# Attention weights normalised by ScalarE, six key heads of eight split

## What is computed

```python
q = rope(rmsnorm(x @ Wq.T))        # 32 query heads of 128, 32 rows per batch element
k = rope(rmsnorm(x @ Wk.T)); v = x @ Wv.T          # 8 key heads
kc = k_cache[block_table].reshape(bsz, 512, 8, 128)  # 16 pages of 32 keys
vc = v_cache[block_table].reshape(bsz, 512, 8, 128)
k_all, v_all = concat(kc, k), concat(vc, v)          # 544 keys
scores = q @ k_all * SCALE                           # 4 query heads share a key head
scores = where(valid, scores, -1e30)
o = softmax(scores) @ v_all
x = x + o @ Wo.T
```

## Time and profile before

| | us |
|---|---|
| median of three runs | 2377.89 (2377.67 to 2379.62) |
| the profiled execution | 2378.1 |
| its span | 2376.3 |
| TensorE busy | 2278.0 (96%) |
| VectorE busy | 1795.4 (76%) |
| ScalarE busy | 1299.5 (55%) |
| GpSimd busy | 1172.7 (49%) |
| normalising by GpSimd (L1089), 512 instructions | 536.3 |
| exponentials by ScalarE (L1193), 512 instructions | 383.8 |
| low halves of the keys by VectorE (L1248), 320 instructions | 260.4 |

### The profile page before, as it was taken

How to read it: one execution, slowest core, us unless ns; L and a number is a source line. 1 busy time by engine, 2 the same in 40 slices (tenths; PEclk the granted TensorE clock), 3 DMA queues, 4 the chain that set the end, 5 groups by cost and what they waited for, 6 DMA issues and landing times. The chain is left out here.

```text
span 2376.3 us, 52345 instructions
## 1 busy us (share of the span) xinstructions
PE 2278.0 (96%) x16384; PEld 1964.1 (83%) x16384; DVE 1795.4 (76%) x3535; ACT 1299.5 (55%) x2647; POOL 1172.7 (49%) x1254
## 2 busy tenths in 40 slices
PE   6889999999995999999999999999999997999998
PEld 6777777777774899999999999999999996888887
DVE  6861799999996788888888888888888886422222
ACT  5632788888874555555555555555555554311111
POOL 5410344444443577777777777777777774000000
PEclk9999999999998899999999999999999998999999
DMA  6633233333324788888888888888888885743442
GB/s 237 219 99 91 75 110 111 111 106 93 111 89 138 254 291 294 290 292 286 291 279 290 287 292 287 299 290 294 278 281 292 290 294 179 226 135 98 127 135 62
DMA packets 447145, 493.28 MB, mean 208 GB/s; under 512 B 95317, under 2 KB 390229, under 8 KB 438742
## 3 DMA queue, kind: packets, MB, share of 16 engines
q1 hardware_dynamic: 410198, 357.98, 47.2%
q0 software_dynamic: 36864, 134.23, 16.1%
HBM read 399.83 MB, written 92.27 MB: 207 GB/s over the span
## 5 line engine op out<-in xcount | busy, mean ns | idle before, releaser
L1089 POOL TENSOR_TENSOR att_probs<-att_probs,att_inverse 128x512 f32<-128x512 f32 x512 | 536.3, 1047 | 287.3 <-DVE att_inverse L1285 282.7
L1193 ACT ACTIVATE att_probs<-att_probs,att_low 128x544 f32<-128x544 f32 x512 | 383.8, 750 | 516.2 <-DVE att_low L1272 451.0
L1150 PE MATMUL att_o<-att_probs_t,att_values 128*128 128x128 f32 x4096 | 540.9, 275 | 0.0
L1272 DVE CUSTOM_DVE_ANT_0 att_probs<-att_score,att_mask,att_batch_cols 128x544 f32<-128x544 f32 x512 | 400.0, 781 | 138.1 <-PE att_score L1115 99.5
L1150 PEld LDWEIGHTS att_o<-att_probs_t,att_values 128*128 128x128 f32 x4096 | 497.7, 192 | 0.0
L1281 DVE COPY att_probs_t<-att_turn 128x512 f32<-128x512 f32 x512 | 350.8, 685 | 1.2 <-PE att_turn L1130 1.2
L1075 POOL DMA_INDIRECT att_values<-L_cond_v_cache,att_v_rows_of x256 | 284.0, 1109 | 82.0 <-POOL att_v_rows_of L1071 49.7
L1115 PE MATMUL att_score<-att_keys_raw,att_queries_raw 128*128 128x288 f32 (+1 forms) x1024 | 290.8, 407 | 28.1 <-DMA att_queries_raw<-q_t 25.9
L1130 PE MATMUL att_turn<-ident,att_probs 128*128 128x128 f32 x2048 | 311.4, 275 | 1.2 <-POOL att_probs L1089 0.9
L784 PE MATMUL proj_proj<-x3t_hi,proj_w_hi 128*128 128x512 f32 x640 | 266.7, 417 | 6.7 <-DVE proj_w_lo L844 6.7
L1248 DVE TENSOR_TENSOR att_keys_lo<-att_keys_raw,att_keys_hi 128x384 fp32r<-128x384 f32 (+1 forms) x320 | 260.4, 814 | 16.7 <-ACT att_keys_hi L1186 16.7
(11 more groups left out here) (133 smaller groups left out, 3982.0 us busy)
## 6 DMA issues: line engine op xcount, KB each, us to landing
att_keys_raw<-L_cond_k_cache SPq DMA_DIRECT2D x1024, 128.0 KB
q_t<-proj_q_out SPq DMA_DIRECT2D x32, 1024.0 KB, 3.9
att_queries_raw<-q_t SPq DMA_DIRECT2D x64, 512.0 KB
o_t<-att_heads_out SPq DMA_DIRECT2D x64, 512.0 KB, 6.7
out_o_raw<-o_t SPq DMA_DIRECT2D x32, 1024.0 KB, 5.6
maps_even<-L_cond_weight SPq DMA_DIRECT2D x8, 1024.0 KB, 12.7
maps_odd<-L_cond_weight SPq DMA_DIRECT2D x8, 1024.0 KB, 16.3
w_nat<-L_cond_Wq SPq DMA_DIRECT2D x8, 1024.0 KB, 5.3
```

Source lines behind the costliest of these rows:

```text
L1089: nc.gpsimd.tensor_tensor(probs[:, k, 0:L], probs[:, k, 0:L], inverse[:, k:k + 1].to_broadcast([P, L]), ALU.mult).then_inc(probs_ready, 1)
L1150: last = nc.tensor.matmul(o, values[j][:, t, h * D:(h + 1) * D], probs_t[m % 2][:, t * P:(t + 1) * P], start=(t == 0), stop=False, skip_gr ...
L1193: nc.scalar.activation(probs[:, k, :], probs[:, k, :], ACT.Exp, bias=low[k][:, 0:1], scale=-1.0, accum_out=total[k][:, 0:1]).then_inc(exp_ ...
L1272: nc.vector.tensor_tensor_reduce(out=probs[:, k, :], in0=score_ps[:, LEFT:LEFT + KEYS], in1=mask[j][:], scale=batch_cols[j][:, h:h + 1], s ...
```

## The change

ScalarE normalises a head's 512 columns, with the inverse as the scale of a copy (`normalise`), behind its high half of that head and ahead of new_part and keep_o. GpSimd keeps the gathers and the new keys' group, for which it waits on the inverse once in four heads. Two heads of a batch element stay native and not four; the six others are split. The halves so hold 6 of 8 heads, the pages are cut into six pieces (five of three pages and one of two), and with the queries there are seven; ScalarE begins with piece 0 behind head 1 and VectorE behind head 2. The release of the keys' buffer follows `NATIVE`.

```diff
--- before.py
+++ after.py
@@ -940,10 +940,10 @@
     GH = 4
     RING = 8
     PAIRS = B // 2
-    NATIVE = 4
-    ACT_FROM, DVE_FROM = 4, 5
+    NATIVE = 2
+    ACT_FROM, DVE_FROM = 1, 2
     SPLIT = HK - NATIVE
-    PARTS = [slice(0, 3), slice(3, 6), slice(6, 9), slice(9, 13), slice(13, NPP + 1)]
+    PARTS = [slice(0, 3), slice(3, 6), slice(6, 9), slice(9, 12), slice(12, 15), slice(15, NPP + 1)]
     NP = len(PARTS)
     FIRST = NPP // 2 + 1
     LEFT = 512 - FIRST * PSIZE
@@ -1084,11 +1084,9 @@
 
                             pool.wait_ge(o_done, i * N + j * HK)
                         load((j + 1) % 2, i * 2 + (j + 1), h - 3)
-                    pool.wait_ge(inverse_ready, i * N + n + 1)
-                    k = n % RING
-                    nc.gpsimd.tensor_tensor(probs[:, k, 0:L], probs[:, k, 0:L], inverse[:, k:k + 1].to_broadcast([P, L]),
-                                            ALU.mult).then_inc(probs_ready, 1)
                     if n % GH == GH - 1:
+                        k = n % RING
+                        pool.wait_ge(inverse_ready, i * N + n + 1)
 
                         heads = slice(k - GH + 1, k + 1)
                         nc.gpsimd.tensor_tensor(new_group[n // GH % 2][:], probs[:, heads, L:KEYS],
@@ -1193,6 +1191,11 @@
                 nc.scalar.activation(probs[:, k, :], probs[:, k, :], ACT.Exp, bias=low[k][:, 0:1], scale=-1.0,
                                      accum_out=total[k][:, 0:1]).then_inc(exp_done, 1)
 
+            def normalise(i, n):
+                act.wait_ge(inverse_ready, i * N + (n + 1))
+                k = n % RING
+                nc.scalar.activation(probs[:, k, 0:L], probs[:, k, 0:L], ACT.Copy, scale=inverse[:, k:k + 1]).then_inc(probs_ready, 1)
+
             def new_part(i, n, first=False):
 
                 m = n % N
@@ -1226,6 +1229,7 @@
 
                             act.wait_ge(scores_done, i * N + j * HK)
                         split(i * 2 + (j + 1), i + j, h - ACT_FROM, (j + 1) % 2)
+                    normalise(i, n)
                     if n % GH == 1 and (n >= GH or not first):
                         new_part(i, n - 2, first)
                     if n % GH == 2 and (n >= GH or not first):
```

## The result

| kernel | median, us | ratio to the kernel before [95%] |
|---|---|---|
| before, same chip | 2378.26 | |
| after | 2527.64 (2524.22 to 2529.38) | 1.0623 [1.0608, 1.0637] |

A forecast was written before the change was run, and what follows sets the result against it. TensorE's list of matmuls was taken as the bound; 2378.1 less 28.8 for the batches, plus 2.2 at the start, less 0.1 at the end, gave 2351.4 us (2351 against the median). Own range 2346 to 2360, wider range 2345 to 2375.

The forecast's parts named there:

- Part 1: TensorE's matmul list: splitting heads 2 and 3 and removing disturbances saves 0.45 us a batch, 28.8 us in 64 batches.
- the loop's end: End of each two-batch loop turn: VectorE's last half shrinks, its mask comes earlier, giving about 0.04 us a batch.
- Part 2: VectorE's low halves: 4032 columns for 2688, undisturbed; 2.06 us a slot against TensorE's shortest 2.09, so they barely fit.
- rival C: Nothing gained: VectorE's 2.06 plus small delays replace TensorE's 2.09; 0.4 us a batch, 2377 us; chance 0.07.
- Part 3: ScalarE's queue: 8 normalisings a batch, each occupying 0.62 us, and 1344 columns of high halves are added at no cost.
- Part 4: Earlier keys: their window shrinks from 20.7 to 18.0 us, landing at 17.1; costs nothing, at worst 2 us late.
- rival A: VectorE halves starting inside a GpSimd gather wait for it: 0.72 us a batch, 2397 us, or 2364; chance 0.16.
- The spare 0.9 us: Margin for keys landing 17.1 us after a batch's first issue, with the first high half at 18.0.
- rival B: Keys land late: each microsecond past the window lengthens every batch by one; 0.3 gives 2370 us; chance 0.14.
- Start: Before head 0 VectorE makes six low halves, 3.8 us where three took 1.50; costs 2.2 us once.
- The sum: Whole kernel: 2378.1 - 28.8 + 2.2 - 0.1 = 2351.4 us for the profiled execution; 2351 against the median.

The follow-up runs named there:

- keys_earlier: keep_first_spaced with the keys' buffer released one head earlier, after head 1 is scored and the last low half made; 2364.26 us, 0.9939.
- gathers_spaced: After, with the second to fourth gather of a batch each waiting for the inverse of the head before it; 2442.01 us, 1.0264.
- keep_first_spaced: After, with new_part and keep_o ahead of normalise on ScalarE and gathers two to four each waiting for an inverse; 2370.26 us, 0.9966.
- start_later: keys_earlier, with the first gather for the second batch element also waiting for an inverse; 2361.67 us, 0.9927.
- gaps: After, with new_part and keep_o ahead of normalise and a GpSimd filler before gathers two to four, no added wait on another engine; 2380.08 us, 1.0005.

## Why the prediction was wrong

**Part 1 (TensorE's list) was right in its mechanism and its size.** Slots h2 and h3 fell to 2.20 and 2.73, within 0.01, in the kernels of the table that split six heads, h6 and h7 to 2.20 and 2.72 once nothing else disturbed them. Mis-sized is only the loop's end: 0.04 a batch was to come back and 0.01 did (h1 2.34 and 2.33). The reason given, a disturbed half of VectorE ahead of the mask, falls: in keys_earlier VectorE stands idle 0.57 there, and the mask is still 0.56 behind the turning.

```profile
1534.90 0.60 PE L1135 MATMUL att_turn<-ident,att_probs 128*128 128x128 f32 x4
```

```profile
1535.46 0.78 DVE L1283 CUSTOM_DVE_ANT_0 att_probs<-att_score,att_mask,att_batch_cols 128x544 f32<-128x544 f32 x1 [0.57 <-PE att_score L1120]
```

**Part 2 (VectorE's halves) was right.** After, by groups (mean ns behind the busy time):

```profile
L1197 ACT ACTIVATE att_probs<-att_probs,att_inverse 128x512 f32<-128x512 f32 x300 | 216.3, 721 | 59.2 <-DVE att_inverse L1289 59.1
...
L1252 DVE TENSOR_TENSOR att_keys_lo<-att_keys_raw,att_keys_hi 128x576 fp32r<-128x576 f32 x187 | 140.1, 749 | 0.0
...
L1252 DVE TENSOR_TENSOR att_keys_lo<-att_keys_raw,att_keys_hi 128x384 fp32r<-128x384 f32 x38 | 20.8, 548 | 0.0
```

Halves of 384 fell from 915 ns to 548. A slot of VectorE with 576 columns takes 2.09 and more in keys_earlier, where 2.06 was reckoned:

```profile
1507.25 0.78 DVE L1283 CUSTOM_DVE_ANT_0 att_probs<-att_score,att_mask,att_batch_cols 128x544 f32<-128x544 f32 x1
...
1507.95 0.68 DVE L1292 COPY att_probs_t<-att_turn 128x512 f32<-128x512 f32 x1
1508.56 0.75 DVE L1259 TENSOR_TENSOR att_keys_lo<-att_keys_raw,att_keys_hi 128x576 fp32r<-128x576 f32 x1
1509.22 0.15 DVE L1296 RECIPROCAL att_inverse<-att_total 128x1 f32<-128x1 f32 x1
1509.34 0.78 DVE L1283 CUSTOM_DVE_ANT_0 att_probs<-att_score,att_mask,att_batch_cols 128x544 f32<-128x544 f32 x1
```

No gap is left in that row of work, so rival C may be there in the small: slot h4 is 2.19 for 2.09. It takes 2.12 in one batch of a pair and 2.24 in the other, where the weighing still stands 0.51 behind its turning for 0.44. So not all of this 0.1 is shown to be VectorE's.

**Part 3 (ScalarE's queue) holds the step that failed first: "Cost nothing; TensorE's list is the cover."** Its sizes stood: the normalising takes 721 ns where 0.72 was taken. (By the figures of the Trainium skill's "ScalarE: Activation LUTs", section "What ACT_TABLE_LOAD costs", the estimate was 0.71; the trace agrees.) It named new_part and keep_o as queued behind the normalising, and then asked only whether ScalarE itself would be late: "It is not late, nor with new_part or keep_o, whose slots are longer". The question left out was who waits for keep_o. It is TensorE, the engine that the text had called the bound, and not two slots later but in the same slot: `weigh` of heads 0 and 4 waits at L1146, in code that the change doesn't touch. The cost put at nothing is 1.21 us a batch in h4 and h0 (gathers_spaced against keep_first_spaced), and 72 us between the medians of these two.

**Part 4 and rival A looked at the three gathers and asked the wrong engine: the second step that failed.** The text saw that three gathers would follow each other ("wanted a batch later") and asked only whether VectorE's halves would wait for them. They don't: the half of 1500.98, shown above, begins inside the gather of 1500.83 and takes 0.75; from 1100 to 1900 us the 37 halves that begin inside a gather take 0.75 in the mean, like the others. (The Trainium skill's "SBUF — State Buffer", section "Who interferes with whom", says that a two-input VectorE instruction contends with a GpSimd instruction that reads SBUF. For GpSimd's elementwise work the trace agrees, 1134 ns for 749; the issue of a gather does not slow the half.) What suffered was something that no row of before's loop could show, since no two gathers stand in a row there: signals of TensorE. Its price, 37 us on top of kind K's cure and 86 without it, had no term in the sum and no rival.

**Part 4 (keys).** The spare 0.9 us was too much. By the records of landings (not all are there), the last of a batch's keys of keep_first_spaced lands 18.1 us behind the first issue in the mean from 1100 to 1900 us, and the first high half comes at 18.4; the forecast had 17.1 and 18.0. The direction of rival B was right, its price 6 us.

**Start.** The 2.2 us for six low halves came (from the first scores to the first mask 2.37 before and 4.51 after). Another 2.3 was missing: a gather that used to stand behind normalisings was set free. That a moved step also unblocks what was queued behind it was written down for the steady loop, not for the start.

**The sum.** With nearly all of both kinds, the late keys and the early gather removed, start_later has 2361.7 us. The batch is 18.77 for 18.59: 0.18 x 64 = 11.5 us, of which h4 is 0.10, h1 0.03 and h0 0.05. The last is two stalls of 1.4 us each, and they are kind G once more. start_later in order of time:

```profile
1298.89 0.99 POOL L1078 DMA_INDIRECT att_values<-L_cond_v_cache,att_v_rows_of  x1 [3.03 <-issue]
...
1300.19 0.94 POOL L1078 DMA_INDIRECT att_values<-L_cond_v_cache,att_v_rows_of  x1 [0.31 <-issue]
...
1301.43 1.23 POOL L1078 DMA_INDIRECT att_values<-L_cond_v_cache,att_v_rows_of  x1 [0.30 <-issue]
...
1303.31 0.60 ACT L1225 ACTIVATE att_heads_out<-att_o 128x512 f32<-128x512 f32 x1 [1.44 <-remote]
```

GpSimd stands still for 3.03 us, and the gathers that it owes then follow each other 1.3 and 1.2 us apart; the turning that ends at 1302.80 is signalled 0.63 late, and keep_o, on ScalarE, waits 1.44 for outputs that are complete at 1301.40. gaps, whose filler stands between the gathers even there, has no such stall. Why GpSimd stands still at these two places isn't known; before loses about 0.54 us in slot h6 of the same two batches. Against the 2351 forecast 10.7 us are left, about what those three slots hold. All that was forecast of the parts was there, but for the 0.1 of h4; what failed is the claim that nothing else changes.

**What stays open.** Why three gathers in a row hold back what TensorE reports. Shown is that a pause of 1 us between them removes it, that it stays with an eighth of the bytes and with half of the rows, and that the copy or mask comes about a microsecond after the third gather. The ends of matmuls in the trace are modelled, so whether the matmuls themselves ended late, or only their signals, can't be told from it. Whether the kernel before, with GpSimd normalising, would show it with gathers moved together wasn't tried.

## What to carry to other kernels

When a step moves into another engine's queue, follow every instruction behind it to the engine that waits for its result, also in code that the diff leaves alone, above all where that engine is the bound; "this engine isn't late" is not an answer. Work that seems in the way may be keeping others apart: before it is taken out, ask what then runs back to back, and put a pause or a wait there. And take the parts one at a time: here each alone was slower, and the two with an order mended by a few lines were 0.7% faster than before.

## What had not been expected of the hardware

Three indirect gathers issued 1.25 us apart on GpSimd delay by up to 2.0 us in after (1.8 at the copy of 1503.86) what VectorE sees of TensorE's finished work, and ScalarE too (keep_o at 1303.31 in start_later); a pair costs little (0.09 us a batch in slot h6), and with gathers 2.1 us or more apart (gaps) no signal was late. A gather of 64 rows occupies GpSimd for the same 0.9 to 1.1 us as one of 128, and with 512 bytes a row for 4 KB the signals are late as well. VectorE's two-input subtraction takes 0.75 us inside a gather and outside.
